# Half of an expert's gate and up products turned round, with the activations transposed behind them

## The chip, the cores and the metric

The kernel runs on one core of one Trainium2 chip. The metric is the time of one execution on the device in microseconds. Its engines are TensorE (PE, with its weight load PEld), VectorE (DVE), ScalarE (ACT), GpSimd (POOL) and SyncE (SP, which here issues transfers only). A queue name with a q (PEq, PEldq, SPq) is an engine's sequencer or the transfers it issues.

## The reference, cut to what matters

A gated cross-attention layer on 32 sequences of 112 tokens (width 256, 8 heads) is followed by a mixture of experts over all 3584 tokens:

```
x = x + tanh(g_xattn) * cross_attention(ctx, layernorm(x), mask)
z = layernorm(x)
bids = sigmoid(z @ conf_w.T + conf_b) * wealth         # 8 experts
combine = softmax over the top 2 bids, 0 for the others
for each expert e:                                       # 1024 hidden units
    y_e = (silu(z @ gate_e.T) * (z @ up_e.T)) @ down_e.T
x = x + tanh(g_ffn) * sum_e combine[e] * y_e
```

The result is kept to f32 accuracy: every f32 operand is split into a high and a low f16 half, and a product is three f16 matmuls (high by high, high by low, low by high) that accumulate in one PSUM bank.

## The kernel before, in words

The attention part (phase A, the first 870 us) writes each token's normalized row twice, sorted by expert, to a buffer in HBM (`routed_rows`). The expert part (phase B) runs over NT = 63 tiles of 128 such rows, in order of experts. Expert weights lie in SBUF (`W2`, five places, high and low halves); which place a tile needs is known only at run time, from a table (`t_exp_i`) that VectorE computes after tile 0. For tiles 0 to 2 the place is the constant 0. From tile 3 on each engine loads the number from the table (`place_of`, line 1592 for TensorE), and TensorE's weight addresses are a register plus an offset (`weights_of`).

TensorE's instructions are written out by hand, with waits on semaphores, in this order for tile t (`step`, line 1600 on):

1. `gate_up(t, .., 0)`: units 0 to 511 of gate into `gP[0]`, of up into `uP[0]`. Four blocks of 128 units each; a block is `product(...)` with KD = 2 row blocks, six matmuls. The weights are the stationary operand (128x128), the tile's transposed rows `xT` move (128 columns). So the outcome has the units on the partitions: `gP[unit, row]`. 48 pairs of weight load and matmul in all.
2. `tile_T(t + 1)`: the rows of the next tile are transposed into `xP` (two f32 transposes), and `expert_sums` in one tile of five.
3. `gate_up(t, .., 1)`: the same for units 512 to 1023, into `gP[1]` and `uP[1]`.
4. the table load for tile t + 1.
5. `down(t - 1)`: 24 matmuls, `aT` of the tile before stationary, the down weights moving (256 columns), into `yP`.
6. waits that the next tile's weights are there (`weights_there`, semaphores `s_wlo` and `s_there`).

Per tile and half i, ScalarE forms `sg[i] = silu(gP[i])`, VectorE `act_h[i] = uP[i] * const * sg[i]` (f32, in SBUF), ScalarE its high half (`act_hi`) and VectorE its low half (`act_lo`) into `aT[q][i]`; with the units on the partitions these are what `down` takes as its stationary operand. Between the two halves ScalarE and VectorE split the next tile's rows (`tile_hi`, `tile_lo`). VectorE then waits for `down(t - 1)` and weighs its rows (`weigh`); GpSimd adds them to the output with an indirect transfer (`add_tile`, line 598), waits until an add has landed, and loads the rows of tile t + 2 (`load_tile`, line 547).

In the first 35 tiles, in groups of SPAN = 5, the next expert is prepared behind that: ScalarE sums squares of six weight pieces (tiles 0 to 2 of a group, two each) and forms high halves (tiles 3 and 4, three each); VectorE forms the low halves (line 1167). Experts 4 to 7 go to HBM and come back into the first four places when those are free, issued by SP (`load_place`). SP also increments `s_there` once by 256, for the four places that are never reloaded before use; in the kernel before that stands behind its second expert load and its last store (line 410).

PSUM has eight banks: `gP`, `uP` two each, `xP`, `yP`, `bP` one each.

Of the kernel before, what the change touches and what calls it, by code (L numbers as in the profile page):

```python
# [54 lines left out]
AHEAD = 4  # L55
assert AHEAD * P * E <= 2 * (TOK - 8 * S)
RELOADS = 4
X_TOP = 2.0 ** 10
A_TOP = 2.0 ** -21
SPAN = 5  # L60
# [21 lines left out]
def build(nc, x, ctxt, mask, scal, lnw, wqkv, wout, confw, confbw, wffn, out):  # L82
# [4 lines left out]
    with ctx:  # L87
# [6 lines left out]
        def psum(name, shape, stack):  # L94
# [154 lines left out]
        yP = psum("yP", [P, 2, D], ppb)[:, 0, :]  # L249
        bP = psum("bP", [P, 512], ppb)  # L250
        uP = [psum(f"uP{i}", [P, 512], ppb) for i in range(2)]
        ppb.close()
        pb.close()

# [34 lines left out]
        s_xt = [sem(f"s_xt{i}") for i in range(4)]  # L289
        s_xtp, s_xthi, s_xtlo, s_gu, s_silu, s_act = [sem(n) for n in (  # L290
            "s_xtp", "s_xthi", "s_xtlo", "s_gu", "s_silu", "s_act")]
        s_athi, s_atlo, s_down, s_yw, s_add = [sem(n) for n in (
            "s_athi", "s_atlo", "s_down", "s_yw", "s_add")]

        def need(eng, semaphore, count):

# [17 lines left out]
        def zseq(b, k):  # L314

            return k if isinstance(b, int) and b == 0 else seq(b - 2, PZ + k)

        def in_place(p):

# [12 lines left out]
        @block.sync  # L332
        def _(sp):
            def load_rows(b, p):

                need(sp, s_z, b - 1)
                need(sp, s_max, H * (b - 4) + 2)
                apart(sp)
                bb = bass.ds(b, 1)
                sp.dma_start(xc[p][:, :, :], ctxt[bb, :, :].rearrange("a (p j) d -> (a p) j d", j=CJ)).then_inc(s_xc[p], 16)  # L340
                sp.dma_start(xl[p][:, :], x[bb, :, :].rearrange("a s d -> (a s) d")).then_inc(s_xc[p], 16)

            def load_mask(b, p):

                need(sp, s_madd, b - 1)
                apart(sp)
                sp.dma_start(mraw[p][:, :], mask[bass.ds(b, 1), :].to_broadcast([S, SC])).then_inc(s_mask[p], 16)

            def load_residual(b, p):

                need(sp, s_x1, b - 1)
                apart(sp)
                sp.dma_start(xres[p][:, :], x[bass.ds(b, 1), :, :].rearrange("a s d -> (a s) d")).then_inc(s_xres[p], 16)

            def store_x1(b, p):
                sp.wait_ge(s_x1, b + 1)
                apart(sp)
                sp.dma_start(out[bass.ds(b * S, S), :], x1[p][:, :]).then_inc(s_x1st[p], 16)

            def turn_of(b, p):  # L360

                if holds(b, 0, B - 1):
                    load_rows(b, p)
                if holds(b, 1, B):
                    load_mask(b - 1, 1 - p)
                if holds(b, 4, B + 3):
                    load_residual(b - 4, p)

                if holds(b, 5, B + 4):
                    store_x1(b - 5, 1 - p)  # L370

            def load_raw(p):

                e = sp.value_load(order_i[0:1, p:p + 1], min_val=0, max_val=E - 1)
                for c in range(PIECES):
                    need(sp, s_wlo, (p - 1) * PIECES + c + 1)
                    sp.dma_start(raw[:, piece_cols(c)],  # L377
                                 wffn[bass.ds(e, 1), :, piece_cols(c)].rearrange("a p c -> (a p) c")).then_inc(s_raw[c], 16)

            for b in range(8):  # L380
                turn_of(b, b % 2)
            with sp.Fori(4, B // 2) as g:
                for k in range(2):
                    turn_of(g * 2 + k, k)
            for b in range(B, B + 2):
                turn_of(b, b % 2)
            sp.wait_ge(s_order, 1)
            sp.wait_ge(s_wready, 2)
            load_raw(0)
            for b in range(B + 2, B + 4):  # L390
                turn_of(b, b % 2)

            def load_place(n):

                step_ = WCOL // RELOADS
                for c in range(RELOADS):
                    sp.dma_start(W2[:, n % SLOTS, :, c * step_:(c + 1) * step_],
                                 wsp[n - SLOTS, :, :, c * step_:(c + 1) * step_]).then_inc(s_there, 16)
                sp.wait_ge(s_there, 16 * RELOADS * (n + 1))

            sp.wait_ge(s_padr, 1)
            for e in range(E):
                r = sp.value_load(pad_row_i[0:1, e:e + 1], min_val=0, max_val=E * CAP - PADT * P)  # L403
                sp.dma_start(xs[bass.ds(r, PADT * P), :].rearrange("(j p) w -> p j w", p=P),  # L404
                             padrows[:, :].unsqueeze(1).to_broadcast([P, PADT, XW])).then_inc(s_padw, 16)

            load_raw(1)
            turn_of(B + 4, 0)

            sp.sem_inc(s_there, 16 * RELOADS * SLOTS)  # L410
            sp.wait_ge(s_tab, 1)
            for n in range(SLOTS, E):

                last = sp.value_load(tile_end_i[0:1, n - SLOTS:n - SLOTS + 1], min_val=0, max_val=NT)
                sp.wait_ge(s_wput, 16 * (n - SLOTS + 1))
                sp.wait_ge(s_down, last + 1)
                apart(sp)
                load_place(n)
            sp.wait_ge(s_x1st[0], 16 * PAIRS)
            sp.wait_ge(s_x1st[1], 16 * PAIRS)  # L420
# [211 lines left out]
        def _(act):  # L632
# [216 lines left out]

            def act_hi(t, q, i):  # L850

                act.wait_ge(s_act, t * 2 + (i + 1))
                need(act, s_down, t)
                nc.scalar.activation(aT[q][i][:, 0, :, :].rearrange("p m s -> p (m s)"), act_h[i][:, :], ACT.Copy).then_inc(s_athi, 1)  # L854

            def step(t, k):
                q = k % 2
                if t < NT:
                    if t == 3:
                        act.wait_ge(s_tab, 1)  # L860
                    place = place_of(t)
                    silu(t, 0, place)
                    act_hi(t, q, 0)
                if t < NT - 1:
                    tile_hi(t + 1, 1 - q)
                if t < NT:
                    silu(t, 1, place)
                    act_hi(t, q, 1)
                p, j = t // SPAN + 1, t % SPAN
                if p < E:  # L870
                    if j < 3:
                        for c in (2 * j, 2 * j + 1):
                            expert_squares(p, c)
                    else:
                        for c in range((j - 3) * 3, (j - 2) * 3):
                            expert_hi(p, c)
                if SLOTS < p <= E and j == 0:
                    put_place(p - 1)

            tile_hi(0, 0)  # L880
            for t in range(NT):
                step(t, t % 4)

        @block.vector
        def _(dve):
# [419 lines left out]
            def gated(t, i, place):  # L1305

                dve.wait_ge(s_silu, t * 2 + (i + 1))
                nc.vector.scalar_tensor_tensor(out=act_h[i][:, :], in0=uP[i][:, :], scalar=constant(place, 2), in1=sg[i][:, :],  # L1308
                                               op0=ALU.mult, op1=ALU.mult).then_inc(s_act, 1)

            def act_lo(t, q, i):
                dve.wait_ge(s_athi, t * 2 + (i + 1))
                nc.vector.tensor_tensor(aT[q][i][:, 1, :, :].rearrange("p m s -> p (m s)"), act_h[i][:, :],  # L1313
                                        aT[q][i][:, 0, :, :].rearrange("p m s -> p (m s)"), ALU.subtract).then_inc(s_atlo, 1)

            def weigh(t, k, place):
# [5 lines left out]
            def step(t, k, place, last_place):  # L1322
                q = k % 2
                p, j = t // SPAN + 1, t % SPAN
                if t < NT:
                    gated(t, 0, place)
                    act_lo(t, q, 0)
                if t < NT - 1:
                    tile_lo(t + 1, 1 - q)
                if p < E and j == 3:  # L1330
                    expert_bound(p, bP)
                if t < NT:
                    gated(t, 1, place)
                    act_lo(t, q, 1)
                if p < E and j == 3:
                    expert_scale(p)
                if t > 0:
# [38 lines left out]
        def _(pe):  # L1376
# [194 lines left out]
            def gate_up(t, q, i, slot_):  # L1571
# [2 lines left out]
                    pe.wait_ge(s_xtlo, t + 1)  # L1574
                need(pe, s_act, (t - 1) * 2 + (i + 1))
                for o, w in ((gP[i], WG), (uP[i], WU)):
                    for m in range(IB // 2):
                        col = w + (i * (IB // 2) + m) * P
                        last = product(o[:, m * P:(m + 1) * P], lambda k, a: weights_of(slot_, a, col + k * I, P),
                                       lambda k, a: xT[q][:, a, k, :], KD)  # L1580
                last.then_inc(s_gu, 1)

            def down(t, q, slot_):

# [14 lines left out]
            def step(t, k, byte, last_byte):  # L1599

                q = k % 2
                if t < NT:
                    gate_up(t, q, 0, byte)
                if t < NT - 1:
                    tile_T(t + 1, (k + 1) % 4)
                if t // SPAN + 1 < E and t % SPAN == 3:
# [6 lines left out]
                if t < NT - 1:  # L1613
                    place = place_of(t + 1)
                    next_byte = byte_of(place)
                if t > 0:
                    down(t - 1, 1 - q, last_byte)
                if t < NT - 1:
# [46 lines left out]
```

## Time and profile before

| | us |
|---|---|
| median of three executions | 1584.86 (1583.99 to 1586.45) |
| the profiled execution, its own time | 1586.34 |
| its span, first to last instruction | 1584.7 |
| mean granted TensorE clock | 0.984 of full |
| TensorE matmul busy | 1439.6 (91%) |
| TensorE weight load busy | 1096.9 (69%) |
| VectorE, ScalarE, GpSimd busy | 1046.5, 942.0, 475.9 |

Busy shares are means over both phases. VectorE and ScalarE are at eight or nine tenths in phase A and at two to five in phase B. Matmuls are pipelined: the profile gives each its full latency (217 ns for 128 columns), so a stream of them is best read by the starts, one group's start to the next one's. In the rows below a number of matmuls is merged into one line as long as engine and line stay the same.

### The profile page before, as it was taken

The numbers are of one execution on the slowest core, as the hardware profiler recorded it, in microseconds if no ns is written. First come the engines' busy times: TensorE is split into PE (matmuls) and PEld (weight loads), VectorE is DVE, ScalarE is ACT, GpSimd is POOL, SyncE is SP. The second block draws the span as 40 slices with busy tenths as digits, with TensorE's granted clock in tenths as the row PEclk, the third lists the DMA queues.
The fourth block names the chain that finished last, engine by engine and source line by source line (L and its number), as shares of the span: only waits on it lengthen the run. The fifth ranks groups of instructions, "written<-read, shape, count | busy, mean of one in ns | idle before, by whom it ended". The sixth has DMA issues, their size and how long they took to land. (4 is left out here: it accounts for less than half of the span.)

```text
span 1584.7 us, 46877 instructions
## 1 busy us (share of the span) xinstructions
PE 1439.6 (91%) x15896; PEld 1096.9 (69%) x15896; DVE 1046.5 (66%) x2552; ACT 942.0 (59%) x1940; POOL 475.9 (30%) x644
## 2 busy tenths in 40 slices
PE   1999999999999999999996799999998999999996
PEld 1566666666666666666665788888787888888875
DVE  4688898898988989889877555445435533333332
ACT  4678777787878778787867454545445422222221
POOL 4232224334243342432413332233222212212211
PEclk9999999999999999999996899999999999999999
DMA  3011011111111010110122542333357231111351
GB/s 114 18 38 38 27 38 42 44 36 50 37 39 50 27 58 24 50 45 29 38 93 75 160 108 38 93 108 120 89 184 237 52 105 26 26 28 26 105 187 15
DMA packets 52198, 107.49 MB, mean 68 GB/s; under 512 B 10704, under 2 KB 32592, under 8 KB 51472
## 3 DMA queue, kind: packets, MB, share of 16 engines
q0 software_dynamic: 20448, 43.13, 11.4%
q1 hardware_dynamic: 29824, 46.70, 9.8%
q10 hardware_dynamic: 1712, 14.70, 2.5%
q8 instruction: 148, 2.42, 0.6%
q14 instruction: 66, 0.54, 0.1%
HBM read 69.16 MB, written 35.34 MB: 66 GB/s over the span
## 5 line engine op out<-in xcount | busy, mean ns | idle before, releaser
L1308 DVE SCALAR_TENSOR_TENSOR act_h<-uP,consts,sg 128x512 f32<-128x512 f32 x126 | 94.6, 751 | 253.0 <-ACT sg L848 252.7
L848 ACT ACTIVATE sg<-gP,consts 128x512 f32<-128x512 f32 x126 | 86.5, 687 | 280.1 <-PE uP L1383 280.0
L1383 PE MATMUL uP<-xT,W 128*128 128x128 f16 x3024 | 250.0, 217 | 0.9
L1383 PE MATMUL fP<-zTs,ws 128*128 128x112 f16 (+1 forms) x1536 | 221.2, 295 | 10.5 <-POOL zTs L479 8.9
L1383 PEld LDWEIGHTS uP<-xT,W 128*128 (+1 forms) x3024 | 209.5, 96 | 29.5 <-issue 4.7
L1383 PE MATMUL gP<-xT,W 128*128 128x128 f16 x3024 | 223.7, 218 | 5.6 <-DVE xT L1302 3.2
L1383 PE MATMUL yP<-W,aT 128*128 (+1 forms) x1512 | 179.3, 275 | 44.8 <-issue 43.9
L1383 PEld LDWEIGHTS gP<-xT,W 128*128 (+1 forms) x3024 | 202.1, 97 | 22.6 <-issue 7.9
L1383 PEld LDWEIGHTS yP<-W,aT 128*128 128x128 f16 x1512 | 144.4, 98 | 71.4 <-issue 52.8
L598 POOL DMA_INDIRECT out<-ysb,xt x63 | 105.2, 1669 | 287.9 <-DVE ysb L1320 266.6
L702 ACT ACTIVATE pr<-ms,nmax 112x488 f32<-112x488 f32 x256 | 179.0, 699 | 15.9 <-DVE nmax L948 14.3
L1383 PE MATMUL fP<-ws,zTs 128*128 128x512 f16 x768 | 187.0, 379 | 0.2
L948 DVE CUSTOM_DVE_ANT_0 ms<-simP,madd,sim_undo 112x488 f32<-112x488 f32 x256 | 184.1, 719 | 3.1 <-PE simP L1431 0.8
L1383 PEld LDWEIGHTS fP<-zTs,ws 128*128 128x128 f16 x1536 | 110.0, 99 | 102.2 <-issue 38.1
L954 DVE SCALAR_TENSOR_TENSOR pT<-ptP,pT 122x448 f16<-122x448 f32 x256 | 158.0, 617 | 20.9 <-ACT pT L709 19.9
L709 ACT ACTIVATE pT<-ptP 122x448 f16<-122x448 f32 x256 | 137.8, 538 | 39.9 <-PE ptP L1441 38.6
L1383 PE MATMUL oP<-v,pT 122*128 122x64 f16 x3072 | 133.5, 194 | 20.4 <-DVE pT L954 17.6
L854 ACT ACTIVATE aT<-act_h 128x512 f16<-128x512 f32 x126 | 79.3, 630 | 118.3 <-DVE act_h L1308 118.3
L1313 DVE TENSOR_TENSOR aT<-act_h,aT 128x512 f16<-128x512 f32 x126 | 87.2, 692 | 87.7 <-ACT aT L854 87.7
L1441 PE MATMUL ptP<-ident,pr 112*122 112x112 f32 x1024 | 142.6, 262 | 0.5 <-DVE filled L1059 0.5
L1383 PEld LDWEIGHTS oP<-v,pT 122*128 122x128 f16 x3072 | 122.7, 98 | 28.9 <-DVE pT L954 28.8
L1441 PEld LDWEIGHTS ptP<-ident,pr 112*122 112x122 f32 x1024 | 115.2, 140 | 25.2 <-issue 1.2
(210 smaller groups left out, 2119.0 us busy)
## 6 DMA issues: line engine op xcount, KB each, us to landing
raw<-wffn POOLq DMA_DIRECT2D x36, 512.0 KB, 7.2
split_experts<-W ACTq DMA_DIRECT2D x4, 3072.0 KB, 10.4
W<-split_experts SPq DMA_DIRECT2D x16, 768.0 KB, 8.0
xc<-ctxt SPq DMA_DIRECT2D x32, 375.0 KB
xt<-routed_rows POOLq DMA_DIRECT2D x63, 129.0 KB, 2.4
raw<-wffn SPq DMA_DIRECT2D x12, 512.0 KB, 9.0
xl<-x SPq DMA_DIRECT2D x32, 112.0 KB
xres<-x SPq DMA_DIRECT2D x32, 112.0 KB, 4.8
```

Of the source, the lines that this page charges most:

```text
L598: pool.indirect_dma_start(out[:, :], bass.IndirectOffsetOnAxis(ap=xt[k][:, D:D + 1].bitcast(I32), axis=0), ysb[k % 2][:, :], None, compute ...
L702: nc.scalar.activation(pr[h % 2][:, :], ms[h % 2][:, :], ACT.Exp, bias=nmax[p][:, h:h + 1], scale=-1.0, accum_out=rsum[p][:, h:h + 1]).the ...
L709: nc.scalar.activation(pT[h % 2][:, 0, :, 0:S], ptP[h % 2][0:KR, :, 0:S], ACT.Copy, scale=P_TOP).then_inc(s_pthi, 1)
L848: nc.scalar.activation(sg[i][:, :], gP[i][:, :], ACT.Silu, scale=constant(place, 0)).then_inc(s_silu, 1)
L854: nc.scalar.activation(aT[q][i][:, 0, :, :].rearrange("p m s -> p (m s)"), act_h[i][:, :], ACT.Copy).then_inc(s_athi, 1)
L948: nc.vector.tensor_tensor_reduce(out=ms[h % 2][:, :], in0=simP[h % 2][0:S, 0:NK], in1=madd[p][:, :], scale=sim_undo[0:S, 0:1], scalar=3.0e ...
L954: nc.vector.scalar_tensor_tensor(out=pT[h % 2][:, 1, :, 0:S], in0=ptP[h % 2][0:KR, :, 0:S], scalar=P_TOP, in1=pT[h % 2][:, 0, :, 0:S], op0 ...
L1308: nc.vector.scalar_tensor_tensor(out=act_h[i][:, :], in0=uP[i][:, :], scalar=constant(place, 2), in1=sg[i][:, :], op0=ALU.mult, op1=ALU.mu ...
L1313: nc.vector.tensor_tensor(aT[q][i][:, 1, :, :].rearrange("p m s -> p (m s)"), act_h[i][:, :], aT[q][i][:, 0, :, :].rearrange("p m s -> p ( ...
L1383: last = nc.tensor.matmul(o, lhs(k, a), rhs(k, c), start=n == 0, stop=n == len(todo) - 1)
L1441: last = nc.tensor.transpose(ptP[h % 2][0:KR, c, 0:S], pr[h % 2][:, c * KR:(c + 1) * KR], ident[0:S, 0:S])
```

## The change

Of the 1024 units of gate and up, only units 0 to 511 (half 0) are computed as before. For units 512 to 1023 (half 1, `TURNED = (1,)`) the operands change places: the tile's rows `xT` are the stationary operand and the weights move, 512 columns at a time. Each of gate and up is one product of six matmuls of 512 columns in place of four products of six of 128 columns. The outcome has the rows on the partitions: `gP[row, unit]`. The silu and the gating are the same instructions on the same shape. What `down` needs has the units on the partitions, so TensorE transposes `act_h[1]` in four f32 transposes of 128x128 into a new PSUM bank `aP` (`act_T`), and the high and low halves are formed from `aP` instead of `act_h[1]`.

The order of the engines changes with it. TensorE's `act_T(t - 1, 1)` stands in tile t, behind `gate_up(t, 0)` and ahead of `tile_T(t + 1)`. ScalarE forms the high half of half 1 in the next tile, behind its first silu, and the high half of half 0 behind `tile_hi`; VectorE accordingly. Both loops get one more step. VectorE's gating gets a wait that the half before it has been consumed. SP increments `s_there` at its start instead of behind its second expert load.

```diff
+TURNED = (1,)
+        aP = psum("aP", [P, 512], ppb)
+        def turned(t, i):
+            return t * len(TURNED) + TURNED.index(i) + 1
 # SP
+            sp.sem_inc(s_there, 16 * RELOADS * SLOTS)
             for b in range(8):
                 turn_of(b, b % 2)
...
             load_raw(1)
             turn_of(B + 4, 0)
-            sp.sem_inc(s_there, 16 * RELOADS * SLOTS)
 # ScalarE
             def act_hi(t, q, i):
-                act.wait_ge(s_act, t * 2 + (i + 1))
+                if i in TURNED:
+                    act.wait_ge(s_at, turned(t, i))
+                else:
+                    act.wait_ge(s_act, t * 2 + (i + 1))
                 need(act, s_down, t)
+                src = aP if i in TURNED else act_h[i]
...
                     silu(t, 0, place)
-                    act_hi(t, q, 0)
+                if t > 0:
+                    act_hi(t - 1, 1 - q, 1)
                 if t < NT - 1:
                     tile_hi(t + 1, 1 - q)
                 if t < NT:
+                    if 0 not in TURNED:
+                        act_hi(t, q, 0)
                     silu(t, 1, place)
-                    act_hi(t, q, 1)
+                    if 0 in TURNED:
+                        act_hi(t, q, 0)
...
-            for t in range(NT):
+            for t in range(NT + 1):
 # VectorE
             def gated(t, i, place):
                 dve.wait_ge(s_silu, t * 2 + (i + 1))
+                if i in TURNED:
+                    need(dve, s_at, turned(t - 1, i))
+                else:
+                    need(dve, s_atlo, (t - 1) * 2 + (i + 1))
...
                     gated(t, 0, place)
-                    act_lo(t, q, 0)
+                if t > 0:
+                    act_lo(t - 1, 1 - q, 1)
                 if t < NT - 1:
                     tile_lo(t + 1, 1 - q)
+                if t < NT and 0 not in TURNED:
+                    act_lo(t, q, 0)
...
                     gated(t, 1, place)
-                    act_lo(t, q, 1)
 # TensorE
                 for o, w in ((gP[i], WG), (uP[i], WU)):
+                    if i in TURNED:
+                        col = w + i * 512
+                        last = product(o[:, :], lambda k, a: xT[q][:, a, k, :],
+                                       lambda k, a: weights_of(slot_, a, col + k * I, 512), KD)
+                        continue
+            def act_T(t, i):
+                pe.wait_ge(s_act, t * 2 + (i + 1))
+                need(pe, s_atlo, t * 2 + i)
+                for m in range(IB // 2):
+                    last = nc.tensor.transpose(aP[:, m * P:(m + 1) * P], act_h[i][:, m * P:(m + 1) * P], ident[:, :])
+                last.then_inc(s_at, 1)
...
                     gate_up(t, q, 0, byte)
+                if t > 0:
+                    act_T(t - 1, 1)
                 if t < NT - 1:
                     tile_T(t + 1, (k + 1) % 4)
```

## Rows read from the trace of the kernel before

**Rows 1.** Busy time by stretch: PE, PEld, DVE, ACT, POOL, clock, DMA, GB/s
```profile
900.00:1560.00 660.00, 613.51 (x7360) 541.92 (x7359) 285.42 (x468) 263.06 (x423) 160.54 (x163) 0.99 0.34 93
```

**Rows 2.** Timeline of TensorE in a steady tile: start, length, what, idle before
```profile
1404.24 1.71 PE L1383 MATMUL gP<-xT,W 128*128 128x128 f16 x24
1405.85 2.02 PE L1383 MATMUL uP<-xT,W 128*128 128x128 f16 x24
1407.79 0.41 PE L1558 MATMUL xP<-ident,xt 128*128 128x128 f32 x2
1408.03 1.91 PE L1383 MATMUL gP<-xT,W 128*128 128x128 f16 x24
1409.88 1.94 PE L1383 MATMUL uP<-xT,W 128*128 128x128 f16 x24
1412.50 2.78 PE L1383 MATMUL yP<-W,aT 128*128 x24 [0.67 <-issue]
```

**Rows 3.** Lines 1383 and 1592 on TensorE's sequencer: ns min/median/max, first and last start
```profile
L1383 PEldq ALU_OP  x101: 32/32/32, 1403.0 to 1416.9; - x101
L1592 PEldq TENSOR_LOAD <-t_exp_i x3: 297/302/312, 1400.8 to 1422.6; - x3
...
L1592 PEldq TENSOR_LOAD <-t_exp_i x3: 302/318/483, 904.5 to 924.8; - x3
```

**Rows 4.** Timeline of TensorE in tiles 2 and 3
```profile
899.89 1.50 PE L1383 MATMUL gP<-xT,W 128*128 128x128 f16 x24 [2.58 <-DVE xT L1302]
...
904.13 1.50 PE L1383 MATMUL uP<-xT,W 128*128 128x128 f16 x24
905.48 2.78 PE L1383 MATMUL yP<-W,aT 128*128 128x256 f16 x24
908.10 1.50 PE L1383 MATMUL gP<-xT,W 128*128 128x128 f16 x24
909.43 1.50 PE L1383 MATMUL uP<-xT,W 128*128 128x128 f16 x24
910.77 0.43 PE L1558 MATMUL xP<-ident,xt 128*128 128x128 f32 x2
```

**Rows 5.** Timeline of TensorE in phase A
```profile
415.93 1.46 PE L1383 MATMUL fP<-ws,zTs 128*128 128x512 f16 x6
417.23 0.55 PE L1441 MATMUL ptP<-ident,pr 112*122 112x112 f32 x4
417.61 0.52 PE L1383 MATMUL oP<-v,pT 122*128 122x64 f16 x12
```

**Rows 6.** Costliest groups: count, busy us, mean ns of one, idle before
```profile
L1308 DVE SCALAR_TENSOR_TENSOR act_h<-uP,consts,sg 128x512 f32<-128x512 f32 x126 | 94.6, 751 | 253.0 <-ACT sg L848 252.7
L848 ACT ACTIVATE sg<-gP,consts 128x512 f32<-128x512 f32 x126 | 86.5, 687 | 280.1 <-PE uP L1383 280.0
...
L854 ACT ACTIVATE aT<-act_h 128x512 f16<-128x512 f32 x126 | 79.3, 630 | 118.3 <-DVE act_h L1308 118.3
L1313 DVE TENSOR_TENSOR aT<-act_h,aT 128x512 f16<-128x512 f32 x126 | 87.2, 692 | 87.7 <-ACT aT L854 87.7
...
L1167 DVE SCALAR_TENSOR_TENSOR W<-raw,escale,W 128x1024 f16<-128x1024 f32 x48 | 59.0, 1279 | 0.5 <-ACT W L806 0.5
```

**Rows 7.** Timeline of GpSimd beside rows 2
```profile
1411.10 0.56 POOL L547 DMA_DIRECT2D xt<-routed_rows  x1 [3.53 <-issue]
```

**Rows 8.** Chain of waits at a weight reload: start, length, what
```profile
1161.82 9.10 DMA out<-ysb,xt
1172.21 3.99 DMA xt<-routed_rows
```

**Rows 9.** Timeline of TensorE at the first tile and the last two down products
```profile
880.74 2.72 PE L1383 MATMUL gP<-xT,W 128*128 128x128 f16 x24 [1.93 <-SPq L410]
...
1565.66 2.93 PE L1383 MATMUL yP<-W,aT 128*128 x24
1569.54 2.85 PE L1383 MATMUL yP<-W,aT 128*128 x24 [0.94 <-DVE ysb L1320]
```

More of the change, by code:

```diff
@@ L291, in build @@
             "s_xtp", "s_xthi", "s_xtlo", "s_gu", "s_silu", "s_act")]
-        s_athi, s_atlo, s_down, s_yw, s_add = [sem(n) for n in (
-            "s_athi", "s_atlo", "s_down", "s_yw", "s_add")]
+        s_at, s_athi, s_atlo, s_down, s_yw, s_add = [sem(n) for n in (
+            "s_at", "s_athi", "s_atlo", "s_down", "s_yw", "s_add")]
         def need(eng, semaphore, count):
@@ L850, in act_hi @@
             def act_hi(t, q, i):
-                act.wait_ge(s_act, t * 2 + (i + 1))
+                if i in TURNED:
+                    act.wait_ge(s_at, turned(t, i))
+                else:
+                    act.wait_ge(s_act, t * 2 + (i + 1))
                 need(act, s_down, t)
-                nc.scalar.activation(aT[q][i][:, 0, :, :].rearrange("p m s -> p (m s)"), act_h[i][:, :], ACT.Copy).then_inc(s_athi, 1)
+                src = aP if i in TURNED else act_h[i]
+                nc.scalar.activation(aT[q][i][:, 0, :, :].rearrange("p m s -> p (m s)"), src[:, :], ACT.Copy).then_inc(s_athi, 1)
             def step(t, k):
@@ L1312, in act_lo @@
                 dve.wait_ge(s_athi, t * 2 + (i + 1))
-                nc.vector.tensor_tensor(aT[q][i][:, 1, :, :].rearrange("p m s -> p (m s)"), act_h[i][:, :],
+                src = aP if i in TURNED else act_h[i]
+                nc.vector.tensor_tensor(aT[q][i][:, 1, :, :].rearrange("p m s -> p (m s)"), src[:, :],
                                         aT[q][i][:, 0, :, :].rearrange("p m s -> p (m s)"), ALU.subtract).then_inc(s_atlo, 1)
@@ L1333, in step @@
                     gated(t, 1, place)
-                    act_lo(t, q, 1)
+                    if 0 in TURNED:
+                        act_lo(t, q, 0)
                 if p < E and j == 3:
@@ L1615, in step @@
                     next_byte = byte_of(place)
+                if t < NT and 0 in TURNED:
+                    act_T(t, 0)
                 if t > 0:
```

## The prediction

> **What bounds the kernel now.** I read the page's shares first, then the busy times by stretch. Steady expert tiles fill 900 to 1560 us, and TensorE is busy there for 613.5 of 660 us at a granted clock of 0.99 [rows 1]: VectorE has 285 and ScalarE 263. So I opened the timeline of one tile [rows 2]. Start to start it reads: gate block 0 1.61 us and up block 0 1.94, the two input transposes 0.24, gate block 1 1.85, up block 1 and what follows it 2.62, the down product 2.62 (905.48 to 908.10 in [rows 4]; the steady one ends up the same); together 10.88 us. The 24 down matmuls of 256 columns are 109 ns apart. The 128-column ones are 67 to 81 ns apart, and before the down product TensorE stands idle for 0.67 us on "issue", that is on its own sequencer.
>
> Is 80 ns the array's rate or the sequencer's? Tiles 0 to 2 address their weights with constants, and there 24 such matmuls with their weight loads take 1.34 us, 56 ns each (904.13 to 905.48, no idle behind it) [rows 4]. Tile 3 uses registers, yet its block 0 runs at 56 ns too (908.10, 909.43, 910.77): it follows a down product with constant addresses, during which the sequencer gets ahead. From tile 5 on both blocks and the down product use registers. The sequencer rows show what that costs: 101 address operations of 32 ns in one and a quarter tiles, and once a tile the load of the next tile's expert number, 302 ns plus register work [rows 3]. In tile 2 that load ran at 904.5, a microsecond before the down product, and left no gap; in the steady tile it stands in the 0.67 us gap. So my reading is that the steady tile is bound by TensorE's sequencer, at about 80 ns a pair, and that the array itself would need 56.
>
> **The change, part by part.**
> Block 1 of gate and of up (units 512 to 1023): 48 pairs of 128 columns go, 12 pairs of 512 columns come. The columns are the same, 6144. The nearest row is six static matmuls of 512 columns, 1.30 us start to start, 217 ns each (415.93 to 417.23) [rows 5]; 12 take 2.60 us. What goes is 1.85 + 1.95 = 3.80. A register address on the moving side may cost the sequencer what it costs on the stationary one, 80 ns a pair, and stays hidden below 217. Bounds for the twelve: 2.56 (four times 53 ns each) and 2.79 (1.46 twice, less what overlaps). I take 2.60.
>
> Activation transposes: four of 128x128 f32 a tile. Four of 112x112 take 0.38 us start to start (417.23 to 417.61) [rows 5], the two of 128x128 0.24 [rows 2]. Four: 0.38 to 0.48; I take 0.45. They stand behind block 0 of the next tile, when what they wait for (the gated activations of block 1) has been ready for over 3 us.
>
> The sequencer. Per tile it now loses 36 pairs at 80 ns (2.9 us) and gains four static pairs and two waits, about 0.3: 10.9 - 2.9 + 0.3 = 8.3 us. The array needs 2.68 (block 0 at 56 ns) + 0.45 + 0.24 + 2.60 + 2.62 = 8.59. So the array becomes the bound, narrowly, and the sequencer gets ahead: during 12 matmuls of 217 ns it gains 12 x 137 = 1.6 us, which covers the 0.7 us of the expert-number load and leaves 0.9; the down product adds about 0.3 (what block 0 of a steady tile shows as its gain, 1.94 - 1.61). Block 0 uses 48 x 24 ns = 1.15 of it. The lead needed is no larger than tile 3 had. Bounds of the tile: 8.3 (below which neither goes) and 9.4 (block 0 stays as it is, 3.55, and only the gap goes). I take 8.65.
>
> One rule of the Trainium skill speaks against this. First the rows: 24 pairs in 1.34 us [rows 4], 6 pairs of 512 columns in 1.30 [rows 5]. "TensorE: Matmul & The Clock Gate", section "Back-to-back issue gap", says that a sustained stream of weight load and matmul pairs is spaced by both, about 81 ns at 128 columns and about 131 ns at 512. By it the block 0 would keep its 80 ns whatever the sequencer does, and block 1 would fall to 12 x 131 = 1.57 us: an estimate of 8.7 us a tile, by another road. The rows deny both figures for this kernel; that steady tiles show 80 is the only agreement.
>
> ScalarE and VectorE. The order changes: gate's block 1 activations are split a tile later, behind the transposes, from PSUM instead of SBUF. Counted from the end of block 0 (T): silu to T+0.8, the transposes end at T+0.45, the f16 copy (630 ns) T+0.8 to 1.45, VectorE's gating (750) to T+1.6, the low half (692) to T+2.3 [rows 6]. The down product starts at T+0.45+0.24+2.60 = T+3.3, so 1.0 us is left, and the copy from PSUM is bounded by silu's 687, which also reads PSUM. Behind the low half on VectorE stand the next input's split and block 0's low half; both are wanted only for the next tile. That cover is thin in the tiles that prepare an expert: two in five of the first 35 have three weight splits of 1279 ns [rows 6] on VectorE after the down product of the tile before (T+5.9). They end at about T+10.3 (5.9, 3.8, and an estimated half microsecond for the weighing ahead of them); the next T is T+8.65, so gating and low half end at T'+3.2 instead of 2.3. That just fits, but the sequencer can't push the down product before it and loses its lead: up to 1 us a tile. I allow 0.4 over 32 tiles, 13 us (0 to 32).
>
> POOL. Its chain: down product done, output rows added, that landed, input rows of the tile after next loaded. The steady tile shows the down product done at 1404.24, the add issued at 1405.97 (1411.10 less 3.53 and the add's 1.60) and the load at 1411.10 [rows 2, 7]. The load must land before the transposes one tile and a half later: 10.9 + 3.55 = 14.4 us after the down product before, 8.65 + 2.68 + 0.45 = 11.8 now. A quiet chain takes 1.7 + 5.1 and at most 4 for the landing, 10.8: no wait. Where expert weights are reloaded it is longer: 9.10 for the add and 3.99 for the load, from 1161.82 to 1176.20, with 1.7 ahead 16.1 [rows 8]. Eight of the 63 are of that kind, with 7.7 to 11.1 us from add to load; each would wait for 1.6 to 5 us, 27 in sum if all land as late. I take 20 (0 to 27).
>
> The edges [rows 9]. The increment of the semaphore for the weight places moves from behind SP's second expert load and last store to its start; TensorE's first tile ended 1.93 us of idle with it. Bounds are 0 and -1.9; its input is split by VectorE only just before, so I take -0.4. Tiles 1 and 2 run at 56 ns already, so their block 1 gains 0.08 and they pay 0.45 for transposes: +0.7. The tile table (some 6 us of VectorE work after tile 0) now stands ahead of tile 0's second split, so the down product of tile 0 falls behind it, but tile 2 waited for the table anyway: 0 to +2, I take 0. At the end the last down product started 3.88 us after the one before; now the transposes come between (2.62 + 0.45, then copy and low half 1.45): 4.55, +0.7. The gating's new waits on VectorE are for work a tile old: nothing.
>
> **Sum.** From tile 3's block 0 (908.10 [rows 4]) to the down product of tile 61 (1565.66 [rows 9]) lie 657.6 us for 60 tiles. After: 60 x 8.65 = 519, + 13 + 20 = 552, so -105.6; edges +1.0. The profiled execution had 1586.34 us (span 1584.7): 1481.7. The median shown is 1.5 lower, so I say 1481.
>
> **The rivals.**
> A, block 0 keeps its 67 to 81 ns because the lead doesn't build or is lost at the waits: 3.55 + 0.45 + 0.24 + 2.60 + 2.62 = 9.46, 568 + 28 of stalls = 596, so 1525. For it: all tiles from the fifth on. Against it: tiles 3 and 4. The skill's rule above, taken for 128 columns alone, is this rival.
> B, the gap of 0.7 stays as well (nothing is pushed past the register load): 10.15, 609 + 12 = 621, so 1550. Against it: 904.5 in tile 2.
> C, stalls behind DMA are double what I take, since the same bytes are moved in less time (adds, loads and raw weights land later): +30, 1510.
> D, slower than before: the down product waits for transposes, copy and low half, and TensorE idles each tile. Its place is the wait ahead of the down product; it decides from a low half that ends 2.3 us after T+3.3, where the tile passes 10.9 again; with the clock halved behind such idles (the first tile's 2.72 against 1.50 [rows 4, 9]) a third of the tiles at double length add 60 x 8.65 / 3 = 173 us: some 1655. Against it: the low half ends at T+2.3 to 3.2, and behind the 2.58 us of idle before tile 2 the 24 matmuls took 1.50 us to the last one's end, as at full clock [rows 4].
>
> **How the numbers follow.** Forecast 0.60 (own range 1465 to 1500), A 0.19, B 0.07, C 0.09, D 0.04, and 0.01 that terms cancel. The range of 8 in 10 reaches over C to A: 1465 to 1527. A measurement of this kernel tells about 0.2% from no change, 3 us; all but D lie far on the fast side: faster 0.95, same 0.01, slower 0.04.
>
> **What would show it.** Steady tiles of 8.6 to 8.8 us, down product to down product; gate and up of block 0 in 1.34 us each; 12 matmuls of block 1 in 2.6; four transposes in 0.45; no idle on "issue" ahead of the down product; waits for the input's DMA at the reloads. Block 0 at 1.6 to 1.9 us would show A, an idle of 0.7 B. The prediction fails if TensorE waits for the low half in quiet tiles.

## The result and the profile after

The changed kernel takes 1493.18 us (median of four, 1488.38 to 1497.75) against 1585.39 for the kernel before: ratio 0.942 (0.939 to 0.945). I had said 1481, 1465 to 1527. Its profiled execution took 1497.75 us, the slowest of the four, with a span of 1496.1; all traces of the changed kernel below are of this one, 4.6 us above the median.

Busy by stretch (PE, PEld, DVE, ACT, POOL, clock, DMA, GB/s), from tile 3's block 0 on, answering to [rows 1]:

```profile
908.34:1470.00 561.66, 533.53 (x5317) 414.99 (x5315) 270.33 (x459) 245.92 (x411) 158.00 (x160) 0.97 0.38 108
```

A quiet tile (one in which no expert is prepared and no input rows come late) of the changed kernel on TensorE, answering to [rows 2]:

```profile
1304.77 1.50 PE L1406 MATMUL gP<-xT,W 128*128 128x128 f16 x24
1306.11 1.56 PE L1406 MATMUL uP<-xT,W 128*128 128x128 f16 x24
1307.63 0.63 PE L1616 MATMUL aP<-ident,act_h 128*128 128x128 f32 x4
1308.09 0.38 PE L1581 MATMUL xP<-ident,xt 128*128 128x128 f32 x2
1308.31 1.46 PE L1406 MATMUL gP<-W,xT 128*128 x6
1309.61 1.46 PE L1406 MATMUL uP<-W,xT 128*128 x6
1310.90 2.78 PE L1406 MATMUL yP<-W,aT 128*128 x24
1313.52 1.50 PE L1406 MATMUL gP<-xT,W 128*128 128x128 f16 x24
```

Start to start: 1.34, 1.52, 0.46, 0.22, 1.30, 1.29, 2.62, 8.75 in sum. The "issue" idle ahead of the down product is gone and block 0, whose instructions did not change, runs at 56 and 63 ns a pair instead of 67 and 81. The median distance of down-product starts over tiles 33 to 61 is 8.72 us, against 10.91 before.

The chain of waits at one place where 3 MB of expert weights are moved (here an expert's halves are written to HBM, `split_experts<-W`, 10.2 us from issue to landing), answering to [rows 8], and TensorE's timeline there:

```profile
1072.56 10.54 DMA out<-ysb,xt
...
1084.70 3.61 DMA xt<-routed_rows
```

```profile
1088.36 0.69 PE L1581 MATMUL xP<-ident,xt 128*128 128x128 f32 x2 [5.11 <-DMA xt<-routed_rows]
1088.84 2.77 PE L1406 MATMUL gP<-W,xT 128*128 x6
1091.39 2.77 PE L1406 MATMUL uP<-W,xT 128*128 x6
```

Busy by stretch there:

```profile
1082.00:1088.36 6.36, 1.25 (x15) 0.95 (x13) 1.35 (x2) 2.21 (x4) 2.19 (x2) 0.94 0.89 296
1088.36:1094.16 5.80, 5.80 (x15) 2.38 (x16) 1.12 (x2) 0.90 (x2) 0.57 (x1) 0.50 0.16 34
```

The input rows come 5.11 us late, and the 12 matmuls behind the idle run at a granted clock of 0.50, that is 1.2 GHz: 5.1 us instead of 2.6. Eight idles of this kind last 1.7 us or more. Four follow the writing out of an expert (5.11, 4.33, 3.09 and 2.70 us), four the reading back of one (2.15, 2.12, 1.72 and 2.05 us). Behind six of them the twelve matmuls run wholly or in part at the lower clock, but the length of the idle does not sort them: behind 3.09 us they run at full clock (1.00 granted), behind 2.15 they don't (0.58 over the next 4.1 us).

```profile
1172.69 0.54 PE L1581 MATMUL xP<-ident,xt 128*128 128x128 f32 x2 [2.15 <-DMA xt<-routed_rows]
1173.03 2.77 PE L1406 MATMUL gP<-W,xT 128*128 x6
...
1194.98 0.44 PE L1581 MATMUL xP<-ident,xt 128*128 128x128 f32 x2 [3.09 <-DMA xt<-routed_rows]
1195.26 1.46 PE L1406 MATMUL gP<-W,xT 128*128 x6
```

The waits of the whole expert part (total, times, longest):

```profile
PE xP L1581 <- DMA xt<-routed_rows: 24.3, 10, 5.1
PE yP L1406 <- DVE aT L1332: 3.7, 7, 1.8
```

From the down product in tile 2 to that in tile 62 there are 60 tiles: 660.2 us before, 571.4 after. Sixty quiet tiles of 8.70 are 522.0. The ten tiles over 9.5 us add 41.8, of which 24 are the waits for input rows, some 14 the half clock behind six of them (the groups' starts against those of a quiet tile), and 1.8 a down product that waits for its low half. All other tiles, almost only those that prepare experts, add 7.5, over half of it in one tile of five (9.3 to 9.5 us).

### The profile page after: what moved, and what is told of

Same layout as the page of the kernel before. It is cut to its first block and busy times, and to the rows that moved or that the text cites. A ratio compares the mean times of both kernels' runs of the same rounds, so it can differ in the third digit from the quotient of the medians.

```text
span 1496.1 us, 41585 instructions
## 1 busy us (share of the span) xinstructions
PE 1367.3 (91%) x13880; PEld 973.6 (65%) x13880; DVE 1036.2 (69%) x2552; ACT 931.4 (62%) x1940; POOL 475.7 (32%) x644
## 5 line engine op out<-in xcount | busy, mean ns | idle before, releaser
L1406 PEld LDWEIGHTS yP<-W,aT 128*128 128x128 f16 x1512 | 148.3, 99 | 42.2 <-issue 10.0
L485 POOL TENSOR_TENSOR zTs<-zT,zTs 128x1200 f16<-128x1200 f32 x32 | 79.2, 2474 | 157.3 <-ACT zTs L689 157.2
L1406 PEld LDWEIGHTS fP<-ws,zTs 128*128 128x128 f16 x768 | 68.0, 98 | 82.0 <-issue 14.4
L1454 PE MATMUL simP<-kT,qT 64*128 64x488 f16 x768 | 101.5, 368 | 11.8 <-DVE nmax L962 8.5
L553 POOL DMA_DIRECT2D xt<-routed_rows x63 | 35.7, 567 | 232.3 <-issue 211.1
L952 DVE SCALAR_TENSOR_TENSOR v<-fP,v 122x512 f16<-122x512 f32 x128 | 88.3, 690 | 27.0 <-ACT v L701 25.8
L952 DVE SCALAR_TENSOR_TENSOR kT<-fP,kT 128x488 f16<-128x488 f32 x128 | 84.8, 663 | 31.7 <-ACT kT L701 31.5
```

The lines of the kernel that those rows point to most:

```text
L485: nc.gpsimd.tensor_tensor(zTs[p][:, 1, :, :], zT[:, :, :], zTs[p][:, 0, :, :], ALU.subtract).then_inc(s_zsplit, 1)
L952: nc.vector.scalar_tensor_tensor(out=o, in0=i, scalar=1.0 / TOP, in1=hi, op0=ALU.mult, op1=ALU.subtract).then_inc(s_plo, 1)
L1406: last = nc.tensor.matmul(o, lhs(k, a), rhs(k, c), start=n == 0, stop=n == len(todo) - 1)
L1454: last = nc.tensor.matmul(simP[i][:, 0:NK], qT[p][r, a, h // 2, :], kT[p][r, c, h // 2, :], start=t == 0, stop=t == len(PARTS) - 1)
```

## The experiments

Eight of the eleven ran on two chips whose kernel before took 1586 and 1587 us. The three with the second half's split first ran on one where it took 1616, so for those the ratio and the length of a tile are compared, not the time. The slower part of that chip's runs lies ahead of the expert tiles: the first down product starts at 923 to 926 us instead of 896.

### The order alone

```diff
-TURNED = (1,)
+TURNED = ()
...
-                if t > 0:
+                if t > 0 and 1 in TURNED:
                     act_T(t - 1, 1)
```

> The changed kernel with nothing turned round (TURNED empty): the new order of ScalarE and VectorE and the earlier increment of the semaphore stay, both halves of gate and up run as 48 pairs of 128 columns, no activation transposes. Theory (the gain is the sequencer's, from 36 fewer register-addressed pairs a tile): no change from before, 1583 to 1588 us, tiles of 10.9 us. Rival (a part of the gain comes from the new order, since halves are split a tile later): 10 to 30 us faster than before.

Measured: 1585.31 us, ratio 0.999 (0.998 to 1.000). The tile is as before, with its gap:

```profile
1347.30 2.85 PE L1406 MATMUL yP<-W,aT 128*128 x24 [0.64 <-issue]
```

So without a turned half the new order and the semaphore are worth at most 0.2%. The gain is that of the turned half.

### The kernel before with constant weight addresses

```diff
+        fixed = sb("fixed", [P, 1024], F16)        # filled with 0.5 at the start
...
-                return W2_bytes[:, bass.ds(byte + (a * WCOL + off) * 2, n * 2)].bitcast(F16)
+                return fixed[:, off % 512:off % 512 + n]
```

> The kernel before with every expert weight address a constant (all products read one small buffer that holds 0.5 everywhere, so the expert outputs are meaningless; waits, loads of the expert number and all other work stay). Same 96 + 24 pairs a tile. Theory (the steady tile is bound by TensorE's sequencer): tiles fall from 10.9 to about 8.2 to 8.3 us (four groups of 1.34, 0.24, 2.62), and the loads behind reloads wait more: 1445 to 1475 us. Rival (128-column pairs with weight loads are spaced at 80 ns in the array itself): no change, 1585.

Measured: 1482.73 us, ratio 0.935 (0.933 to 0.936). Not one matmul fewer, and it is as fast as the changed kernel. One tile:

```profile
1341.20 1.50 PE L1385 MATMUL gP<-xT,fixed 128*128 128x128 f16 x24
1342.54 1.50 PE L1385 MATMUL uP<-xT,fixed 128*128 128x128 f16 x24
1343.88 0.39 PE L1560 MATMUL xP<-ident,xt 128*128 128x128 f32 x2
1344.11 1.50 PE L1385 MATMUL gP<-xT,fixed 128*128 128x128 f16 x24
1345.45 1.50 PE L1385 MATMUL uP<-xT,fixed 128*128 128x128 f16 x24
1346.79 2.78 PE L1385 MATMUL yP<-fixed,aT 128*128 128x256 f16 x24
1349.41 1.50 PE L1385 MATMUL gP<-xT,fixed 128*128 128x128 f16 x24
```

8.21 us: every group of 24 pairs in 1.34, weight loads included. The edit also puts one small buffer in the place of the weights. That this is not what makes the pairs faster is shown by tiles 0 to 2 of the kernel before, which read the weights themselves at constant addresses and take the same 1.34 us [rows 4]. This settles it: the 80 ns of the kernel before are the sequencer's, not the array's. The time is above my 1445 to 1475 because waits for input rows grow to 39 us with the shorter tile:

```profile
PE xP L1560 <- DMA xt<-routed_rows: 39.2, 15, 5.6
```

The Trainium skill ("TensorE: Matmul & The Clock Gate", section "Back-to-back issue gap") states about 81 ns a pair at 128 columns and about 131 at 512 for a sustained stream. The first fits the kernel before, but as the rate of its register-addressed pairs. At constant addresses the array does a pair in 56 ns, each with its weight load, and one of 512 columns takes 216; no run here shows 131, and the measurements decide.

### The changed kernel with constant weight addresses

The same edit on the changed kernel.

> The changed kernel with constant weight addresses in the same way. Theory (the array is now the bound, the sequencer ahead in most tiles): little to gain, quiet tiles 8.6 instead of 8.7, 3 to 12 us faster than the changed kernel, 1481 to 1490. Rival (the changed kernel is still bound by the sequencer, only less): a gain of over 20 us.

Measured: 1482.46 us, ratio 0.935 (0.933 to 0.936), some 12 us below the changed kernel (by the ratios). Down products:

```profile
1303.95 2.78 PE L1408 MATMUL yP<-fixed,aT 128*128 128x256 f16 x24
1312.51 2.78 PE L1408 MATMUL yP<-fixed,aT 128*128 128x256 f16 x24
1321.06 2.78 PE L1408 MATMUL yP<-fixed,aT 128*128 128x256 f16 x24
```

8.55 us a tile is what the array needs (1.34 + 1.34 + 0.44 + 0.22 + 2.59 + 2.62 = 8.55). The changed kernel's 8.70 is 0.15 above it, 9 us over 60 tiles.

### One activation transpose instead of four

```diff
-                for m in range(IB // 2):
+                for m in range(IB // 2 if t == 0 else 1):
                     last = nc.tensor.transpose(aP[:, m * P:(m + 1) * P], ...
```

> The changed kernel with one activation transpose a tile instead of four from the second tile on (three quarters of the second half's activations stay those of tile 0). Theory (array bound): 0.33 us a tile less, 20 us over 60 tiles, of which waits for input rows give a few back: 1474 to 1482. Rival (sequencer bound): six instructions of some 27 ns less, 0.16 us a tile, of which nothing shows where it is ahead: 1483 to 1493.

Measured: 1491.79 us, ratio 0.940 (0.938 to 0.942); the median quiet tile is 8.73. My theory fell here: 0.33 us of array work a tile went and nothing was gained. So the quiet tile is not bound by the array. The timeline shows block 0's second group slower instead, and the low half it depends on:

```profile
1304.39 1.79 PE L1406 MATMUL uP<-xT,W 128*128 128x128 f16 x24
1306.09 0.30 PE L1616 MATMUL aP<-ident,act_h 128*128 128x128 f32 x1
...
1306.32 0.69 ACT L854 ACTIVATE sg<-gP,consts 128x512 f32<-128x512 f32 x1 [5.00 <-PE uP L1406]
...
1306.90 0.59 ACT L864 ACTIVATE aT<-aP 128x512 f16<-128x512 f32 x1
1307.16 0.75 DVE L1326 SCALAR_TENSOR_TENSOR act_h<-uP,consts,sg 128x512 f32<-128x512 f32 x1 [3.25 <-ACT sg L854]
...
1307.83 0.68 DVE L1332 TENSOR_TENSOR aT<-aP,aT 128x512 f16<-128x512 f32 x1
```

The copy from `aP` waits for the silu ahead of it on ScalarE, and the low half for the gating on VectorE, with one transpose as with four. Hence a second theory: the sequencer can't pass the down product's wait before the low half (2.4 us after the end of block 0), and from there to the end of the next block 0 its own rate counts. The rival: 8.70 is just the sum of what it issues.

The sequencer's own rows in the changed kernel's trace bear the theory out. In the quiet tile shown in the section on the result it has loaded the next expert number and finished the register work by 1309.5, and there is no further address operation (`ALU_OP`) before 1310.0, where the low half ends (1309.32 + 0.68). A tile later the first one comes at 1318.7, and the low half ends at 1318.71. The rows of the two stretches, from 1309.3 and from 1318.0 on:

```profile
L1406 PEldq ALU_OP  x9: 32/32/32, 1310.0 to 1311.0; - x9
...
L1406 PEldq ALU_OP  x11: 32/32/32, 1318.7 to 1319.9; - x11
```

From 1310.0 on they come, with one pause of 0.6 us, up to 1316.1, just before the array ends block 0 at 1316.3: the sequencer has no lead left there. The matmuls show no idle for it, since the array still has block 1 to do while the sequencer stands.

### The second half's split first

```diff
+                if t > 0:
+                    act_hi(t - 1, 1 - q, 1)
                 if t < NT:
                     silu(t, 0, place)
-                if t > 0:
-                    act_hi(t - 1, 1 - q, 1)
...                                   # act_lo and gated on VectorE likewise
```

> The changed kernel with the second half's high and low halves formed ahead of the next tile's silu and gating, so that the low half ends about 0.6 us earlier after block 0. Theory W (the quiet tile of 8.70 us is a loop: TensorE's sequencer can't push the down product before the low half, and so has too little lead for block 0): quiet tiles 8.56 us, the array's own sum, and fewer long tiles where experts are prepared: 1478 to 1488. Rival S (8.70 is simply the sum of what the sequencer issues in a tile): no change in quiet tiles, 1490 to 1494.

Measured: ratio 0.937 (0.935 to 0.939), 1514.01 us on the slower chip. Quiet tiles are 8.55 to 8.57 us:

```profile
1335.17 0.62 PE L1617 MATMUL aP<-ident,act_h 128*128 128x128 f32 x4
...
1336.46 0.69 DVE L1333 TENSOR_TENSOR aT<-aP,aT 128x512 f16<-128x512 f32 x1 [3.10 <-ACT aT L864]
```

The same two in the changed kernel:

```profile
1316.29 0.63 PE L1616 MATMUL aP<-ident,act_h 128*128 128x128 f32 x4
...
1318.03 0.68 DVE L1332 TENSOR_TENSOR aT<-aP,aT 128x512 f16<-128x512 f32 x1
```

From the first transpose to the end of the low half it is 1.98 us instead of 2.42, and the 0.15 us a tile is gone: the second theory holds. The sequencer's address operations go on 0.3 us earlier too, 2.1 us after the first transpose instead of 2.4. First to last down product takes 573.5 us against 586.3 for the changed kernel; over the whole time the interval of this ratio touches that of the changed kernel's (both have 0.939 as an end), so it is the tile that shows the gain.

> The same with one activation transpose a tile instead of four from the second tile on (most of the second half's activations stay those of tile 0). Array sum 8.56 less 3 x 0.11 = 8.23. W: quiet tiles between 8.23 and 8.5, whichever of the array and the sequencer's own sum is longer; the tile then shows that sum. S: 8.70 again, as with one transpose and the old order.

Measured: ratio 0.933 (0.930 to 0.935), 1506.32 us on the slower chip. Quiet tiles 8.22 to 8.46, median 8.36: with the early low half and three transposes fewer, the tile comes to lie between the array's 8.23 and the 8.5 I had set as the upper end. The low half now ends 1.73 us after the first transpose, but the sequencer's address operations go on only at 2.1, when the load of the next expert number and its register work are done. So here that load holds the sequencer and no longer the low half; 2.1 instead of 2.4 is the 0.3 by which the tile is shorter than 8.70.

### Both halves turned round

```diff
-TURNED = (1,)
+TURNED = (0, 1)
```

> The changed kernel with both halves turned round: 24 pairs of 512 columns and eight activation transposes a tile. Theory (a tile takes the longer of array and sequencer; array here 24 x 0.216 + 8 x 0.11 + 0.22 + 2.62 = 8.9 us, sequencer some 5 to 6): quiet tiles 8.9 us against 8.7, stalls behind reloads a little smaller: 1498 to 1508. Rival (the sequencer is what counts, the array has room): faster than the changed kernel, under 1485.

Measured: 1498.73 us, ratio 0.945 (0.943 to 0.947), quiet tiles 8.89: the array's sum. The rival is out; a sequencer with time to spare doesn't help once the array bounds the tile. Half the units turned is better than none and no worse than all.

### Input rows loaded ahead of the add's wait

```diff
-        xt = [sb(f"xt{i}", [P, XW], F32) for i in range(AHEAD)]
+        xt = [sb(f"xt{i}", [P, XW], F32) for i in range(NX)]          # NX = 6
 # GpSimd, step t
-                if holds(t, 2, NT):
-                    pool.wait_ge(s_add, t * 16 - 16)
-                if holds(t, AHEAD - 2, NT - 3):
-                    load_tile(t + 2, (k + 2) % 4)
+                if holds(t, 3, NT):
+                    pool.wait_ge(s_add, t * 16 - 32)
+                if holds(t, AHEAD - 3, NT - 4):
+                    load_tile(t + 3, (t + 3) % NX)
+                if holds(t, 2, NT):
+                    pool.wait_ge(s_add, t * 16 - 16)
```

> The changed kernel with six buffers for input rows instead of four: the rows of tile t+3 are loaded before the wait for the output add of tile t-2, which only the next add still needs. Theory (what the changed kernel loses beyond its quiet tiles is that the input rows come late behind slow adds, 24 us of waits in its trace, and the half clock that follows them): the waits of the two transposes go, 1460 to 1473. Rival (the reloads slow the tiles in another way, by instruction fetch or by weight pieces that ScalarE waits for): 1483 to 1493.

Measured: 1467.70 us, ratio 0.925 (0.924 to 0.927): 25 us below the changed kernel, no wait for input rows left. Its waits:

```profile
ACT junk L806 <- DMA raw<-wffn: 31.0, 16, 6.9
PE yP L1410 <- DVE aT L1336: 11.6, 5, 3.0
```

What remains where weights are moved is ScalarE waiting for weight pieces and, behind it, the split that the down product needs.

> The kernel before with the same six buffers and early loads. Both theories: its tiles of 10.9 us cover the slow adds already (one wait of 1.0 us in its trace), 1582 to 1587. If it gains over 5 us, the loads were a cost before too.

Measured: 1583.00 us, ratio 0.998 (0.997 to 0.999), 3 us. Late input rows cost the kernel before next to nothing; the shorter tile uncovered them.

> The kernel before with constant weight addresses (reading one buffer of 0.5, outputs of the experts meaningless) and the six buffers with early loads. Theory (with fixed addresses it has quiet tiles of 8.20 us, below the changed kernel's 8.70, and loses the difference to later input rows, 39 us of waits): the waits go, 1430 to 1450. Rival (a tile is not much shorter than 8.7 in the long run because another engine sets the pace): 1465 to 1483.

Measured: 1442.70 us, ratio 0.910 (0.908 to 0.911), quiet tiles 8.21. The rival is out.

> The changed kernel with both: the halves formed first, and six buffers for input rows with early loads. W: quiet tiles 8.56 and no waits for input rows: 1455 to 1463, faster than the early loads alone (1467.7). S: 1465 to 1469.

Measured: ratio 0.919 (0.917 to 0.921), 1484.45 us on the slower chip; quiet tiles 8.55. It is the best version that computes everything, ahead of the early loads alone by 0.6% (their intervals are apart); first to last down product 544.4 us against 554.0. The absolute range I gave, 1455 to 1463, was for the other chips; 0.919 of their 1586 is 1458.

## Why the prediction was right, and where it wasn't

- The bound before (sequencer, 80 ns a register-addressed pair, 56 for the array) was right, shown by constant addresses. It was read from the tiles at the start whose addresses were constants.
- 12 matmuls of 512 columns: 2.59 us against 2.60. Transposes: 0.44 to 0.46 against 0.45. The gap: gone. Block 0: 2.68 to 2.86 against 2.68. Quiet tile: 8.70 against 8.65.
- "So the array becomes the bound, narrowly" was wrong: its sum is 8.55, and the tile 8.70 is held by the sequencer behind the low half, as its own rows and the reordered splits show and the removed transposes confirm. The size was right for a wrong reason, which is luck: two bounds lie 0.15 us apart. The sign of failure that I had named, TensorE waiting for the low half in quiet tiles, does not show as idle of the matmuls; it is the sequencer that waits. I had counted the sequencer at 8.3 without the wait it can't pass, though I had named that wait for the tiles that prepare experts.
- Preparing experts: 13 us said, 7.5 measured.
- "I take 20 (0 to 27)" for the reloads is the term that was mis-sized: 42 us. The waits alone are 24, near the 20, and eight of them are of the size said. But behind six of the eight the clock is at its lower level for 3 to 6 us, which costs some 14 us in all and which I had priced only in the rival that ends slower. I had leaned on the idle of 2.58 us before tile 2 that left the clock full [rows 4]. Here idles of 2.05 to 2.70 us did not, while one of 3.09 did, so one row was too little to go by; what decides it stays open. Half of the eight, and 15 of the 24 us, stand beside the writing out of an expert and not beside a reload. Early loads won 25 us back.
- The sum: I set 60 x 8.65 for a stretch that is one down product short of sixty tiles, 2.6 us too much. With quiet tiles +3, preparation -5.5 and the tiles over 9.5 us +21.8 that makes the +16.8 of the stretch (568.8 us against 552) but for 0.1. The profiled time is 16.1 above my 1481.7, so the edges came to +0.2 instead of +1.0.
- The edges: TensorE's first tile no longer waits for the semaphore of [rows 9] but for its input's split, and starts 1.27 us earlier, of which 0.95 already lies ahead of the input's transposes, so 0.3 against my 0.4. The last down product comes 4.71 us after the one before, where I had 4.55. But from its start to the end of the span it is 14.3 us instead of 15.2, which no term of mine has and no run explains. Tile 0's down product did fall behind the tile table, as said: it waits 2.88 us and then takes 4.46 us at the lower clock instead of 2.78, and tile 3 still starts only 0.24 us later than before (908.34 against 908.10).

The first tile and the last two down products:

```profile
879.47 2.72 PE L1406 MATMUL gP<-xT,W 128*128 128x128 f16 x24 [1.61 <-DVE xT L1316]
...
1477.11 2.78 PE L1406 MATMUL yP<-W,aT 128*128 x24
...
1481.82 2.78 PE L1406 MATMUL yP<-W,aT 128*128 x24 [1.49 <-DVE aT L1332]
```

## What to carry to other kernels

Where matmul addresses come from registers, compare the spacing with that of the same matmuls at constant addresses before believing it is the array's; fewer and wider matmuls, even with transposes to pay for, then gain more than their columns tell. When a loop gets shorter, look for the round trip through another queue whose slack was the old length, and price the clock behind each new idle. A wait in TensorE's stream can cost its sequencer the lead even where the matmuls show no idle. To find what holds a tile, remove a piece of each candidate: one that gives nothing back is not it.

## What the hardware showed that I had not expected

The load of a number from SBUF into a register of TensorE's sequencer took 302 ns before [rows 3]. In the quiet tiles of the changed kernel its median is 497:

```profile
L1628 PEldq TENSOR_LOAD <-t_exp_i x17: 298/497/600, 1256.2 to 1396.0; - x17
```

With one transpose it is 301 again, with both halves turned 299, with the split first 416, with the split first and one transpose 489. Since the tile with one transpose is no shorter, and the load is over before the low half ends, this is not what holds the changed kernel's tile; why the load takes longer stays open.
